# One of three first-layer parts in three float32r passes, with GpSimd making the low halves

## The reference, cut to what matters

```python
emb = tables[feat_idx, sparse]                     # 2048 x 26 x 32
xk = x0 = emb
for w, bb in ((conv1_w, conv1_b), (conv2_w, conv2_b)):
    hp = einsum('bhd,bmd->bhmd', xk, x0).reshape(-1, h * M, E)
    xn = sigmoid(einsum('oi,bid->bod', w, hp) + bb)
    xk = xn[:, :half]; res.append(xn[:, half:])
# cin_out from res, summed over the 32 components; then a deep part:
h1 = tanh(deep_x @ W1 + b1); h2 = tanh(h1 @ W2 + b2); h3 = tanh(h2 @ W3 + b3)
```

## Time and profile before

| | us |
|---|---|
| runs | 1583.1, 1586.48, 1590.08; median 1586.48 |
| the profiled execution | 1593.15 |
| its span | 1591.3 |

### The profile page before, as it was taken

One profiled execution on the slowest core, in us unless ns is written; L12 is line 12 of the kernel. 1 busy time (PEld: TensorE's weight loads), 2 busy tenths in 40 slices (PEclk: granted clock), 3 DMA queues, 4 the chain that ended last, 5 costly groups with the idle time before them and its releaser, 6 DMA issues.

```text
span 1591.3 us, 23672 instructions
## 1 busy us (share of the span) xinstructions
PE 1515.7 (95%) x6552; PEld 661.8 (42%) x6552; DVE 1152.5 (72%) x1113; ACT 646.6 (41%) x904; POOL 686.5 (43%) x600
## 2 busy tenths in 40 slices
PE   0599999999999999999999999999999999999999
PEld 0233333333333333333333333333333337787876
DVE  3278788888888888878787888888888685344442
ACT  2344344443444444344434344444443323444443
POOL 7538574637464655546454646374731110000000
PEclk9999999999999999999999999999999999999999
DMA  6688788988899888989998989998999983846741
GB/s 132 136 217 214 204 220 230 218 232 210 233 202 236 217 235 208 239 202 241 192 237 205 245 205 236 217 242 211 238 220 233 223 226 96 196 125 167 176 127 53
DMA packets 177869, 322.08 MB, mean 202 GB/s; under 512 B 30160, under 2 KB 106032, under 8 KB 177796
## 3 DMA queue, kind: packets, MB, share of 16 engines
q1 hardware_dynamic: 140989, 294.37, 72.0%
q10 hardware_dynamic: 23534, 20.23, 5.7%
q0 software_dynamic: 13312, 7.06, 4.7%
HBM read 300.24 MB, written 21.31 MB: 202 GB/s over the span
## 4 chain that ended last, share of the span: by engine, by line
PE 82%; DMA 5%; SPq 3%; DVE 3%; POOL 3%; issue 3%; ACT 1%; ACTq 0%; DVEq 0%; POOLq 0%
PE acc L834 39%; PE acc L828 19%; PE bc L971 14%; PE bc L814 5%; DMA xb<-x_rows 3%; PE bc L821 3%; POOL emb L604 3%; SPq L511 2%; DVE xb L781 2%; SPq L522 1%; DMA emb<-table,idx_stage 1%; DVE hp L781 1%; PE bc L806 1%; DMA x_halves<-deep_halves 0%; ACT sq L1013 0%
## 5 line engine op out<-in xcount | busy, mean ns | idle before, releaser
L604 POOL DMA_INDIRECT emb<-table,idx_stage x416 | 484.4, 1164 | 319.0 <-DVE hp L781 161.7
L781 DVE TENSOR_TENSOR hp<-bc,xk 128x1024 f32<-128x1024 f32 x384 | 446.2, 1217 | 215.5 <-PE bc L814 180.6
L781 DVE TENSOR_TENSOR xb<-xb,xk 128x1024 f32<-128x1024 f32 x448 | 570.9, 1329 | 20.1 <-DMA xb<-x_rows 19.9
L834 PE MATMUL acc<-xb,w2s 128*64 128x512 f32 x1792 | 410.5, 595 | 3.1 <-DVE xb L781 2.6
L834 PE MATMUL acc<-hp,w2s 128*64 128x512 f32 x1536 | 360.4, 604 | 0.0
L828 PE MATMUL acc<-sq,w1s 128*128 128x512 f32 x768 | 351.4, 607 | 2.9 <-ACT sq L1013 2.2
L1013 ACT ACTIVATE sq<-bc 128x1024 f32<-128x1024 f32 x192 | 182.9, 1027 | 231.0 <-PE bc L821 231.0
L834 PEld LDWEIGHTS acc<-xb,w2s 128*64 128x64 f32 x1792 | 126.4, 137 | 258.9 <-issue 218.2
L615 POOL TENSOR_TENSOR r<-r 128x512 f32<-128x512 f32 x96 | 134.0, 1395 | 220.9 <-ACT r L1020 114.2
L828 PEld LDWEIGHTS acc<-sq,w1s 128*128 128x128 f32 x768 | 142.1, 192 | 182.7 <-issue 181.2
L834 PEld LDWEIGHTS acc<-hp,w2s 128*64 128x64 f32 x1536 | 99.2, 137 | 195.3 <-issue 168.0
(11 more groups left out here) (61 smaller groups left out, 812.7 us busy)
## 6 DMA issues: line engine op xcount, KB each, us to landing
xb<-x_rows SPq DMA_DIRECT2D x448, 256.0 KB, 6.0
xb<-x_rows SPq DMA_DIRECT2D x192, 512.0 KB, 4.9
w_raw<-W SPq DMA_DIRECT2D x48, 512.0 KB, 3.6
xb<-x_rows SPq DMA_DIRECT2D x128, 128.0 KB
x0t<-x_halves ACTq DMA_DIRECT2D x252, 52.0 KB
x_full<-x_halves SPq DMA_DIRECT2D x96, 128.0 KB
emb<-table,idx_stage POOLq DMA_INDIRECT x416, 4.3
x_halves<-deep_halves SPq DMA_DIRECT2D x16, 384.0 KB, 6.1
```

The lines of the kernel that those rows point to most:

```text
L604: nc.gpsimd.indirect_dma_start(out=emb[:, m, :], out_offset=None, in_=table, in_offset=bass.IndirectOffsetOnAxis(ap=idx_stage[:, m:m + 1], ...
L781: nc.vector.tensor_tensor(product(n)[:, :], x[:, :], xk[sl % 2][:, :], ALU.mult).then_inc(multiplied, 1)
L834: last = nc.tensor.matmul(acc_y[H * c:H * c + H, :], w2s[:, ORDER[n], :], src[:, c * CHUNK:(c + 1) * CHUNK], start=(n == 0), stop=(n == PA ...
```

## The change

- The first of the three parts (`HALVED = 1`) is contracted in float32r: ScalarE writes its square twice, in full to `sq` (signal `sq_full`) and rounded to `sq_hi` (signal `squared`), GpSimd subtracts the two to `sq_lo` (`lower_squares`, 128x1024, once a step), and `contract_k` runs high by high, low weights by high and high weights by low, instead of one float32 matmul. For c = 0 it waits for `sq_low` ahead of the third pass. The weights' halves are made once at the start, by ScalarE and VectorE.
- `lower_squares` stands in GpSimd's queue at each step, ahead of gathers or between gathers and adds. In tile 0 the first gathers stand otherwise around it, and four gathers of tile 2 are taken out of the later list and put in step 1.
- `keep_busy` runs 7 float32 matmuls of 13x512, whose result isn't used, while TensorE waits for the first `x0t`, and 3 more ahead of tile 0's first fill of products.
- `load_x` for the first deep group is cut into eight equal parts, one behind the spreads of each step of tiles 14 and 15, the last step too.
- `orow` shares memory with `h_raw[0]`.

```diff
+HALVED = 1
+        sq_lo = [sc(f"sq_lo{k}", [P, COLS], F32R) for k in range(HALVED)]
+        sq_hi = [sc(f"sq_hi{k}", [P, COLS], F32R) for k in range(HALVED)]
...
-                    if ahead == 1:
-                        if sl == 0:
-                            sp.wait_ge(dense_dumped, 64)
-                        load_x(0, sl, 4 * STEPS)
-                    if ahead == 0 and sl < STEPS - 1:
-                        load_x(0, 1 + sl, STEPS)
+                    if ahead == 1 and sl == 0:
+                        sp.wait_ge(dense_dumped, 64)
+                    if ahead < 2 and not is_first:
+                        load_x(0, (1 - ahead) * STEPS + sl, 2 * STEPS)
...
+            def lower_squares(s):
+                for k in range(HALVED):
+                    pool.wait_ge(sq_full, halved_by(s, k))
+                    pool.wait_ge(squared, squared_by(s, k))
+                    nc.gpsimd.tensor_tensor(sq_lo[k][:, :], sq[k][:, :], sq_hi[k][:, :], ALU.subtract).then_inc(sq_low, 1)
...
-                    gather(range(8), gathered)
-
-                    for m, (signal, count) in enumerate(((k_contracted, 1), (xk_made, 1), (xk_made, 2), (squared, K1 + 1),
-                                                         (squared, K1 + 2), (squared, 2 * K1))):
+                    gather(range(6), gathered)
+                    lower_squares(-1)
+                    gather(range(6, 8), gathered)
+
+                    for m, (signal, count) in enumerate(((k_contracted, 1), (xk_made, 1), (xk_made, 2), (squared, K1 + 1))):
                         pool.wait_ge(signal, count)
                         hold()
                         gather((8 + m,), gathered)
-                    gather_in(s, range(14, M), (0, 1, 2, 3, 4, 4, 4, 4, 5, 6, 7, 8))
+                    lower_squares(s)
+                    gather_in(s, range(12, 24), (0, 0, 0, 1, 2, 3, 4, 4, 4, 4, 5, 6))
+                    lower_squares(s + 1)
+                    gather_in(s, range(24, M), (7, 8))
                     add_up(t, 1, r1, r1_step, xn_read, 2, sum1)
                     add_up(t, 2, r1, r1_step, xn_read, 2, sum1)
                     free_emb(t + 1, filled_by(t, DEEP_STEP, ("D", DEEP_N - 1), ahead))
+                    lower_squares(s + 2)
+                    gather_in(s + 1, range(4), (7, 8, 10, 12))
                     add_up(t, 1, r2, r2_step, y2_read, 1, sum2)
-                    gather_in(s + 2, range(5), (1, 2, 3, 4, 6))
+                    gather_in(s + 2, range(4, 9), (1, 2, 3, 4, 6))
                     add_up(t, 3, r1, r1_step, xn_read, 2, sum1)
-                    gather_in(s + 2, range(5, 11), range(7, PAIRS))
+                    lower_squares(s + 3)
+                    gather_in(s + 2, range(9, 15), range(7, PAIRS))
                     add_up(t, 2, r2, r2_step, y2_read, 1, sum2)
-                    gather_in(s + 3, range(11, 22), (0, 1, 1, 2, 3, 3, 4, 5, 6, 7, 7))
+                    gather_in(s + 3, range(15, 22), range(7))
                     return
+                lower_squares(s)
                 if ahead > 0:
                     gather_in(s - 1, range(22, M), (8, 9, 10, 12))
                 add_up(t - 1, STEPS - 1, r2, r2_step, y2_read, 1, sum2)
                 add_up(t, 1, r1, r1_step, xn_read, 2, sum1)
+                lower_squares(s + 1)
                 if ahead > 1:
                     free_emb(t + 1, filled_by(t, 1, ("D", DEEP_N - 1), ahead))
                     gather_in(s + 1, range(4), (0, 2, 4, 6))
                 add_up(t, 2, r1, r1_step, xn_read, 2, sum1)
+                lower_squares(s + 2)
...
                 add_up(t, 3, r1, r1_step, xn_read, 2, sum1)
+                if ahead > 0:
+                    lower_squares(s + 3)
...
-            def contract_k(c, acc_k):
+            def contract_k(c, acc_k, s):
                 cols = slice(c * CHUNK, (c + 1) * CHUNK)
-                for k in range(K1):
-                    last = nc.tensor.matmul(acc_k[:, :], w1s[:, k, :], sq[k][:, cols], start=(k == 0), stop=(k == K1 - 1))
+                halved = [(w[:, k, :], sq_hi[k][:, cols]) for k in range(HALVED) for w in (w1_hi, w1_lo)]
+                halved += [(w1_hi[:, k, :], sq_lo[k][:, cols]) for k in range(HALVED)]
+                full = [(w1s[:, k, :], sq[k][:, cols]) for k in range(HALVED, K1)]
+                passes = halved + full if c == 0 else full + halved
+                for i, (w, x) in enumerate(passes):
+                    if c == 0 and i == 2 * HALVED:
+                        pe.wait_ge(sq_low, halved_by(s, HALVED - 1))
+                    last = nc.tensor.matmul(acc_k[:, :], w, x, start=(i == 0), stop=(i == len(passes) - 1))
...
+            pe.wait_ge(deep_loaded, DEEP_LOADED)
+            def keep_busy(n, acc_free):
+                for _ in range(n):
+                    nc.tensor.matmul(acc_free[:, :], idf[0:ND, :], dense_rows[:, 0:CHUNK], start=True, stop=True)
+            keep_busy(7, acc[0])
...
+                        if start and kind == "fill" and what[0] == 0:
+                            pe.wait_ge(xn_read, 2)
+                            keep_busy(3, acc[1])
...
             def square(k, slot):
-                nc.scalar.activation(sq[k][:, :], bc[slot][:, :], ACT.Square).then_inc(squared, 1)
+                if k < HALVED:
+                    nc.scalar.activation(sq[k][:, :], bc[slot][:, :], ACT.Square).then_inc(sq_full, 1)
+                    nc.scalar.activation(sq_hi[k][:, :], bc[slot][:, :], ACT.Square).then_inc(squared, 1)
+                else:
+                    nc.scalar.activation(sq[k][:, :], bc[slot][:, :], ACT.Square).then_inc(squared, 1)
```

More of the change, by code:

```diff
@@ L216, in build @@
         bias_out = sb("bias_out", [P, 1])
-        orow = sb("orow", [P, CHUNK])
         bias1 = sb("bias1", [P, 1])
@@ L246, in build @@
         sq = [sc(f"sq{k}", [P, COLS]) for k in range(K1)]
+        sq_lo = [sc(f"sq_lo{k}", [P, COLS], F32R) for k in range(HALVED)]
+        sq_hi = [sc(f"sq_hi{k}", [P, COLS], F32R) for k in range(HALVED)]
+        w1_hi = sc("w1_hi", [P, HALVED, P], F32R)
+        w1_lo = sc("w1_lo", [P, HALVED, P], F32R)
         hp = [sc(f"hp{i}", [P, COLS]) for i in range(len(BY_PE))]
@@ L264, in build @@
         h_raw = [sb(f"h_raw{i}", [P, CHUNK]) for i in range(2)]
+        orow = h_raw[0]
         h_hi = sb("h_hi", [P, HIDDEN, CHUNK], F32R)
@@ L310, in build @@
         squared = sem("squared")
+        sq_full = sem("sq_full")
+        sq_low = sem("sq_low")
+        w1_high = sem("w1_high")
+        w1_low = sem("w1_low")
         multiplied = sem("multiplied")
@@ L344, in squared_by, with halved_by @@
             return s * K1 + (K1 + k + 1)
+        def halved_by(s, k):
+            return s * HALVED + (HALVED + k + 1)
         def multiplied_by(s, n):
@@ L751, in _ @@
                 lower_deep(ks)
+            dve.wait_ge(w1_high, 1)
+            nc.vector.tensor_tensor(w1_lo[:, :, :], w1s[:, 0:HALVED, :], w1_hi[:, :, :], ALU.subtract).then_inc(w1_low, 1)
             for i, fields in enumerate(FIRST_FIELDS):
@@ L875, in _ @@
                 spread_sum(k, k, x0t[0])
-            pe.wait_ge(w1_step, W1_STEPS)
+            pe.wait_ge(w1_low, 1)
             pe.wait_ge(squared, K1)
             for c in range(2):
-                contract_k(c, first_acc(-1, c))
+                contract_k(c, first_acc(-1, c), -1)
             pe.wait_ge(w2_loaded, W2_LOADED)
@@ L929, in tile @@
                                 pe.wait_ge(y2_read, s)
-                            contract_k(what, first_acc(sl, what))
+                            contract_k(what, first_acc(sl, what), s)
                         elif kind == "terms":
@@ L1029, in _ @@
                 turned_deep(i, i)
+                if i == 0:
+                    act.wait_ge(w1_step, W1_STEPS)
+                    nc.scalar.activation(w1_hi[:, :, :], w1s[:, 0:HALVED, :], ACT.Copy).then_inc(w1_high, 1)
             act.wait_ge(first_halves, FIRST_HALVES)
```

## The result

| | us |
|---|---|
| after, median of 4 runs | 1643.01 (1642.31 to 1645.55) |
| before, median of 4 runs beside it | 1587.91 (1583.1 to 1590.08) |
| ratio, 95% interval | 1.0353 [1.0319, 1.0386] |
| profiled execution after, its span | 1643.17, 1641.4 |

The account below looks back on a forecast made before the run. TensorE was taken as the bound before, VectorE's chain after. Repeated steps +32, start -1.8, loads -4 and tiles 14 and 15 -1.1 sum to +25: profiled 1618, median 1612 us, range 1588 to 1632.

Parts of the forecast that it names:

- The main term: In the repeated steps, GpSimd's subtraction collides with VectorE's products 8 to 12, which read SBUF twice: 2.2 us a step.
- the term of +32: The 51 repeated steps, from tile 1 to tile 14's first, take 1020.2 us instead of 988.1.
- The start: Everything up to the row that starts step 5 (175.6 us): net -1.8 us, bounds -6 and +3.
- the loads: End of the loop: halving the lumps of nine loads on SP's queue saves 4 us, bounds 0 and -7.
- `keep_busy` should prevent that: Tile 0: no lower clock from 67.5 to 73 and no slow first `contract_k`, some 4 us gained.
- I expect those transposes 2.5 later, near 96.: Tile 0: transposes that wait for the last gathers, delayed by three subtractions queued ahead on GpSimd.
- this wait should go: -5.7.: Tile 1: TensorE's 3.96 us wait for gathers, 164.8 to 168.76, and the lower clock after it disappear, saving 5.7.
- tile 14 and the rest of tile 15 (-1.1): Few gathers and adds there, so steps stay at TensorE's 18.7: -0.35 in some steps, -1.1 us in all.
- Missing the streak: Rival: the subtraction falls outside products 8 to 12, VectorE pays nothing, TensorE stays the bound; 1562 us, chance 0.13.
- The late queue: Rival: GpSimd's last gathers miss step 1's transposes by 2 to 4 us each tile; 1638 to 1662, chance 0.10.

Follow-up runs that it names:

- e1: Changed kernel with GpSimd's subtraction replaced by two memsets of `sq_lo`, the low half of the squares left out; 1633.2 us, ratio 1.0236 (one run).
- e4: Changed kernel with the subtraction on VectorE ahead of product 0 instead of on GpSimd; 1598.1 us, ratio 1.0035.
- e6: e4 without `keep_busy` and with the gathers of fields 12 and 13 gated as before the change; 1581.6 us, ratio 0.9962.
- e10: Changed kernel, no `keep_busy`, old gates; subtraction after product 12, ahead of gathers waiting for it; `sq_lo` pass last in the first half; 1621.6 us, ratio 1.0178.
- e14: e6 with the changed kernel's gates again: gathers of fields 12 and 13 wait for product 0; 1584.2 us, ratio 0.9976.
- e11: e6 with SP's transfers for the deep layers as before the change; 1591.3 us, ratio 0.9974.
- e12: e6 with `keep_busy` back, each of its matmuls replaced by four of 128 rows and 128 columns; 1595.3 us, ratio 1.0009.
- e5: Changed kernel with the gathers of fields 12 and 13 waiting for squares as before, one subtraction behind them; 1643.2 us, ratio 1.0344.

## Why the prediction was wrong

**The main term was right.** The clash of the subtraction with the double-SBUF products, 2.2 a step, makes VectorE the bound: gap before product 0 at 1.70, `xb` at 1601 ns (forecast about 1.65 us), `hp` unchanged, TensorE down to 93% and waiting for `xb`. Steps 1, 2 and 3 were forecast at 19.8, 20.6 and 19.8 and took 19.80, 20.61 and 19.78. Step 0 was put at 19.8 and took 20.20: 12 times 0.4 is more than the 3.6 by which the term of +32 fell short of +35.6. e1 takes the clash away and the streak is 7.64 again; e4 and e6 take the subtraction off GpSimd and every undisturbed step is shorter than before the change, save step 3 (19.4 for 19.0). TensorE's saving, 0.35 a step, is in all of them (18.69). The subtraction itself was put at 2.35 alone and took 2.39 where it met no product that reads SBUF twice.

**The step that failed is "The start".** It said: -1.8 at 175.6, bounds -6 and +3. It was +14.5. That is 16.3 of the 25 us by which the span missed the forecast; the loads and tile 15 are 4.1, the loop 3.6, the rest 1.0. The part of it that doesn't hang on single executions is step 1 of tile 0, 11 us longer than before. The -1.8 is 2.5 and 1.4 later less 5.7; the 4 us that `keep_busy` was to bring aren't in it.
- "`keep_busy` should prevent that ... brings tile 0 some 4 us ahead." It cost 3.5 at tile 0's first fill (71.1 for 67.6): the first call took 12.31 us, each instruction 0.88, twice the 0.44 of the earlier trace rows, and held the spreads back from 51.0 to 53.5; the second took 4.03, and the granted clock at 71 to 76 was still 0.54. I had not costed its own instructions.
- "I expect those transposes 2.5 later, near 96." They came at 103.9, with a wait of 7.21. I counted the subtractions ahead of the last gathers, but not that two gathers now wait for product 0 instead of squares, in a queue whose rest is issued back to back up to the last one. Behind that wait the lower clock came (0.59 at 104 to 111), so step 1 of tile 0 took 32.9 us for 21.8. Without `keep_busy`, with the gates of before and no subtraction right ahead of the last two gathers the transposes come at 94.2 to 96.8 in five kernels of six (e10: 100.1). How much of it is the gates' isn't shown.
- "this wait should go: -5.7." It went (no wait ahead of tile 1's transposes), but `sq_lo` was 2.75 late there at 168.44, behind four gathers, and step 4 took 25.9 as before (25.6). With the subtraction on VectorE it is 19.8 in e6 and e14, but 25.1 to 25.8 in e4, e11 and e12, where TensorE waits for ScalarE instead. So step 4 can't be put down to GpSimd's queue alone.

**The loads:** -4 was put on halving the lumps. With tile 14 and the rest of tile 15 (-1.1) it gave -1.0. e11 and e6 show that the wait moves a tile ahead.

**The rivals.** Missing the streak (1562): it didn't happen by itself, and made to happen it doesn't give 1562: with the subtraction past product 12 GpSimd's queue makes `sq_lo` late. The late queue was thus real, at +26 to +50 in my text, but through `sq_lo` and in the start, not through each tile's transposes; in the changed kernel's loop it is nearly absent (TensorE waits 7.7 us for `sq_lo` in the whole run).

## What to carry to other kernels

A subtraction on GpSimd is not free because GpSimd is idle 57% of the time: here it had to fall where VectorE doesn't read SBUF twice, and every instruction behind it in the queue moved. Before costing a moved gather, list what each later one waits for and whether the queue has any slack up to the last of them; where it is issued back to back, a wait at its head can reach its end (in e5 the gates of before sent fields 12 and 13 3.0 us earlier, and the last gather 1.0). The work that a warm-up issues is itself on the path of the engine that it warms. And before a difference between two profiled executions is given to an edit, look at what the same program does twice: here the start alone moved by 8 us.

## What the runs showed of the hardware that I had not expected

- Matmuls of 13 rows without a gap for 12.31 us never left the slow pace (0.88 for each instruction of 512 columns), and the spreads behind them took 1.65 for six, as without them; with 128 rows and as many columns it was 7.81 and 0.98. The granted clock stands at 1.00 in both stretches, so at the very start of the trace the durations, not that column, told the pace.
- A wait of TensorE of 4.40 us cost 1.7 more behind it (5.28 for 3.59, clock 0.62).
- In e1 VectorE began product 0 at a tile's end 2.5 us after its fill was there (654.03 against 651.5, "remote" as the releaser). In e11 VectorE stood for 7.61 and ScalarE for 9.43 in step 4, with the same releaser, and TensorE then waited 3.34 for ScalarE. Why stays open.
